# Moving the transposes of x between the scores and the output product in a decoupled cross-attention kernel

## The reference

```python
q = heads(x @ W_q);  k_t = heads(text @ W_k);  v_t = heads(text @ W_v)
probs_t = softmax(q k_t^T * scale)                       # over 73 text tokens
text_out = probs_t @ v_t
qsem = l2norm(probs_t @ text);  sem = qsem @ l2norm(ip)^T # over the 1024 context columns
probs_ip = softmax(q k_ip^T * scale + 0.5 * sem) * spatial_mask   # over 4 image tokens
out = (text_out + probs_ip @ v_ip) @ W_out + b_out + x
```

## Time and profile before

| | us |
|---|---|
| median of 3 runs (lowest, highest) | 1042.71 (1041.78, 1043.53) |
| the profiled execution | 1040.03 |
| span of its trace, first to last instruction | 1038.2 |
| TensorE busy | 981.1 |
| VectorE busy | 806.9 |
| ScalarE busy | 707.7 |
| GpSimd busy | 641.9 |
| busy time of all 16 DMA engines in queue q1 | 84.3% |

### The profile page before, as it was taken

One profiled execution on the slowest core, in us unless ns is written; L12 is line 12 of the kernel. 1 busy time (PEld: TensorE's weight loads), 2 busy tenths in 40 slices (PEclk: granted clock), 3 DMA queues, 4 the chain that ended last, 5 costly groups with the idle time before them and its releaser, 6 DMA issues.

```text
span 1038.2 us, 24562 instructions
## 1 busy us (share of the span) xinstructions
PE 981.1 (95%) x7604; PEld 791.6 (76%) x7604; DVE 806.9 (78%) x2401; ACT 707.7 (68%) x2315; POOL 641.9 (62%) x1899
## 2 busy tenths in 40 slices
PE   7986778999999999999999999999999999999877
PEld 5755666888877888888877888888878888888755
DVE  4375678888978788888878888888868888887851
ACT  1354778777677777777766777777767787777720
POOL 1112467777676677667666767767756677676750
PEclk9988999999999999999999999999999999999989
DMA  9845988979799998888899989798889989679852
GB/s 292 325 129 133 192 160 157 165 169 186 160 191 178 186 190 172 172 169 169 156 200 180 186 172 182 156 187 167 164 179 193 177 172 184 138 158 150 161 116 74
DMA packets 483871, 180.26 MB, mean 174 GB/s; under 512 B 449517, under 2 KB 461855, under 8 KB 483740
## 3 DMA queue, kind: packets, MB, share of 16 engines
q1 hardware_dynamic: 483708, 178.62, 84.3%
q10 hardware_dynamic: 32, 0.07, 0.0%
HBM read 42.34 MB, written 27.22 MB: 67 GB/s over the span
## 4 chain that ended last, share of the span: by engine, by line
PE 76%; DMA 5%; DVE 3%; ACT 2%; SPq 2%; issue 2%; POOL 1%; POOLq 0%; DVEq 0%; ACTq 0%
PE ps_O L1149 25%; PE ps_Q L1183 25%; PE ps_S L1122 12%; PE ps_U L1169 11%; DMA pts<-ph 5%; PE ps_M L1199 3%; ACT pr L905 2%; SPq L825 1%; SPq L795 0%; ACT ph L917 0%; DVE smax L1014 0%; DVE pr L1060 0%; DVE n L1072 0%; SPq L785 0%; DVE bias L1021 0%
## 5 line engine op out<-in xcount | busy, mean ns | idle before, releaser
L905 ACT ACTIVATE pr<-ps_S,bias 128x73 f32<-128x73 f32 x1280 | 290.1, 339 | 130.4 <-DVE bias L1021 129.8
L987 POOL TENSOR_TENSOR ph<-pr,ph 128x220 f16<-128x220 f32 (+1 forms) x640 | 273.6, 460 | 153.4 <-ACT ph L917 153.3
L1149 PE MATMUL ps_O<-wo_hi,aT 128*128 128x320 f16 x1280 | 297.2, 303 | 5.6 <-DVE x_in L1006 3.5
L1183 PE MATMUL ps_Q<-xT,wq_hi 128*128 128x512 f32 x800 | 282.4, 418 | 6.8 <-DVE qT L994 6.5
L917 ACT ACTIVATE ph<-pr 128x292 f16<-128x292 f32 x640 | 234.2, 440 | 5.1
L1149 PE MATMUL ps_O<-wo_lo,aT 128*128 128x320 f16 x640 | 193.4, 302 | 0.0
L1169 PE MATMUL ps_U<-xm,pts 128*128 128x110 f16 (+1 forms) x2560 | 159.7, 213 | 20.6 <-DMA pts<-ph 17.6
L1149 PEld LDWEIGHTS ps_O<-wo_hi,aT 128*128 128x128 f16 x1280 | 126.0, 98 | 64.1 <-DVE x_in L1006 4.1
L1183 PEld LDWEIGHTS ps_Q<-xT,wq_hi 128*128 128x128 f32 x800 | 147.8, 193 | 34.8 <-DVE qT L994 8.1
L1169 PEld LDWEIGHTS ps_U<-xm,pts 128*128 128x128 f16 (+1 forms) x2560 | 144.6, 98 | 38.6 <-issue 14.5
L1122 PE MATMUL ps_S<-kbd,qT 128*128 128x308 f32 x960 | 168.5, 311 | 5.2 <-ACT pr L905 5.1
(11 more groups left out here) (185 smaller groups left out, 1273.2 us busy)
## 6 DMA issues: line engine op xcount, KB each, us to landing
out_dram<-x_in SPq DMA_DIRECT2D x64, 320.0 KB, 2.6
x_in<-in_x_dram SPq DMA_DIRECT2D x56, 320.0 KB, 3.2
pts<-ph SPq DMA_TRANSPOSE x320, 3.4
aT<-in_L_xattn_W_k_dram SPq DMA_DIRECT2D x5, 512.0 KB, 8.7
w_ip<-in_L_xattn_W_k_ip_dram SPq DMA_DIRECT2D x1, 2560.0 KB, 11.6
w_v<-in_L_xattn_W_v_dram SPq DMA_DIRECT2D x1, 2560.0 KB, 19.5
w_ip<-in_L_xattn_W_v_ip_dram SPq DMA_DIRECT2D x1, 2560.0 KB, 9.4
x_in<-in_x_dram SPq DMA_DIRECT2D x2, 1280.0 KB, 12.4
```

Of the source, the lines that this page charges most:

```text
L905: last = nc.scalar.activation(pr[p % P_RING][:, j, h, :], sc[:, j, h, 0:T], ACT.Exp, bias=bias[p % 2][:, j, h:h + 1], scale=SCALE)
L987: nc.gpsimd.tensor_tensor(lo, full[:, :, t0:t1], one[:, :, 0, t0:t1], ALU.subtract).then_inc(pl_ready, 1)
L1149: last = nc.tensor.matmul(o_bank[half % 2][:, 0:HALF], stationary, moving, start=(k, a, b_) == O_MMS[0], stop=(k, a, b_) == O_MMS[-1])
L1183: last = nc.tensor.matmul(ps_Q[:], wq[a][:, c, k * P:(k + 1) * P], xT[(CC * i + c) % XT_RING][b_][:], start=(c, a, b_) == Q_MMS[0], stop=( ...
```

## The change

TensorE's transposes X move from the end of a step to the place right behind S and ahead of O. ScalarE and VectorE take them out of `ps_M` in the same step p instead of p+1. The chunks c = 3 and 4 are placed one step later in the table, so that their copies stay in the steps they were in; the chunks 0, 1, 2 keep their steps, so that their copies come a step earlier.

```diff
-    XT_AT = {-10: 0, -9: 1, -8: 2, -4: 3, -3: 4}
+    XT_AT = {-10: 0, -9: 1, -8: 2, -3: 3, -2: 4}
@@ scalar engine
-                for j, c in x_at(p - 1):
+                for j, c in x_at(p):
                     act.wait_ge(xT_ready, CC * j + c + 1)
@@ tensor engine, step p
                     last.then_inc(s_ready, 1)            # end of S
+                for j, c in x_at(p):
+                    if j == 0 and c < X_EARLY:
+                        continue
+                    if c == 0:
+                        pe.wait_ge(x_loaded[j % X_RING], ...)
+                    if j:
+                        if m_free is not None:
+                            pe.wait_ge(*m_free)
+                        m_free = xT_lo, CC * j + c + 1
+                    for q in range(SUB):
+                        last = nc.tensor.transpose(x_bank(j, c)[:, q * P:(q + 1) * P],
+                                                   x_in[j % X_RING][:, q, c * P:(c + 1) * P], ident[:])
+                    last.then_inc(xT_ready, 1)
                 for i, half, piece in out_at(p):         # O
...
                         last.then_inc(q_ready, 1)        # end of Q
-                for j, c in x_at(p):
-                    (the same block)
```

More of the change, by code:

```diff
@@ L1125, in _ @@
                     last.then_inc(s_ready, 1)
+                for j, c in x_at(p):
+                    if j == 0 and c < X_EARLY:
+                        continue
+                    if c == 0:
+                        pe.wait_ge(x_loaded[j % X_RING], 16 * (SUB * (j // X_RING + 1) if j % X_RING > 1 else SUB * (j // X_RING) + 1))
+                    if j:
[6 more added lines that the diff above has]
+                    last.then_inc(xT_ready, 1)
                 for i, half, piece in out_at(p):
```

## The result

The changed kernel takes 1032.39 us (median of 4, 1031.25 to 1034.81) against 1042.99 us (median of 4, 1041.78 to 1043.53): ratio 0.9912, 95% interval 0.9892 to 0.9931. It is 10.6 us faster where 1.8 were forecast. The profiled execution took 1031.25 us, with a span of 1029.5.

A forecast was written before the change was run, and what follows sets the result against it. TensorE bounds it, full from 180 to 940 us and often waiting from 97 to 180. Start -1.2, changes of batch -0.9, late S +0.3 make -1.8 us: 1042.7 to 1040.9 us, range 1037.3 to 1045.5.

The forecast's parts named there:

- The base: From 180 to 940 us: TensorE busy 752.2 of 760 us, its only sizeable wait U's for `pts`, 7.7 us.
- that execution lay 2.7 us under the median of the runs: Remark in the sum: the profiled execution took 1040.03 us, the median 1042.7.
- Rival B: Steps 1 and 7: new order makes GpSimd's instruction hold `bias`, S(63) waits 0.5 us, 7.5 us lost, 1048; chance 0.15.
- They miss each other by more than now: Argument against a slower kernel: in step 1 `bias` comes 0.09 us earlier while GpSimd isn't earlier.
- Gain 1: Start, 97 to 180 us: X and copies moved out of the chain gain 1.2 us, bounds 0 and 2.0.
- Gain 2: Changes of batch: X goes ahead of U's wait in steps 40 and 82, 0.44 us each, 0.9 us; bounds 0 and 0.9.
- a wait which I had priced at nothing: Tile load, needed 5 us earlier: if late by 1 or 2 us in step 80, X waits before a waiting U; nothing.
- What stayed hidden: Every tile: S loses cover, 0 to 0.1 us a tile; ScalarE's and VectorE's copies and the tile load cost nothing.
- the 0.3 put down: Step 66 to 67: S some 0.1 us late behind the exponentials in such tiles; 0.3 us in all, ends 0 and 1.5.
- 0.4 us of cover: Step 62 on ScalarE: free at 443.1 after X's copy and two others, `bias` comes at 443.54.
- Rival A: Start: earlier X shortens waits so one or two TensorE clock falls vanish, about 1 us each; 1038.2, chance 0.17.

The follow-up runs named there:

- before_no_reload: Kernel before without the loads of keys and values for batches 1 to 3 and TensorE's waits for them: 0.9924, 1035.3 us against 1042.6.
- before_psum3: Kernel before with `smax` in PSUM instead of SBUF only in steps that end in 3: 0.9949, 1036.5 us against 1041.3.
- the first two experiments: Both kernels rerun unchanged (0.9991, 0.9914); then chunks 0, 1, 2 a step earlier in the kernel before (1.0001), a step later in the changed one (0.9923).
- before_psum: Kernel before with `smax` in unused PSUM columns instead of SBUF in all steps: 0.9958, 1032.4 us against 1038.2.
- split_34: Only chunks 3 and 4 moved behind S, chunks 0, 1, 2 as in the kernel before: 1.0000 of the kernel before, and 0.9990 when run again.
- before_psum_all: Kernel before with `smax` in PSUM in all steps, run again on another chip: 0.9933, 1034.2 us against 1041.3.
- before_psum7: Kernel before with `smax` in PSUM instead of SBUF only in steps that end in 7: 0.9957, 1038.1 us against 1041.3.

## Why the prediction was wrong

**The base.** The step that failed is the first one: "TensorE is simply full, and its only wait of size is U's for `pts`", which made the long regime worth nothing. That held for the execution in the profile and not for the kernel. In other executions Q of step 7 waits 0.36 us for a `qT` that stands behind a held `bias`, in ten or eleven tiles, at 0.77 us a tile: 8 us that the sum had at nothing. Of the four profiles with this order and with `smax` in SBUF in every step, two have tiles of 55.5 us (1040.0 and 1037.1 us in all) and two of 56.3 (1044.4 us, and before_no_reload). There was a faint sign in the prediction itself, "that execution lay 2.7 us under the median of the runs"; but on the next chip single executions of the kernel before ran from 1038.2 to 1047.5 us, so 1040.0 was nothing unusual, and only a second profile could tell. The hold of step 7 is not the whole gain either: the execution of 1040.0 us, which has none, still took 7.6 us more than the changed kernel's median of 1032.4.

**Rival B, the right mechanism with the wrong sign.** It weighed the lock only as something that the change might switch on. The change switches it off. "They miss each other by more than now" was said of step 1, where it did not come true: the median distance from `bias` to GpSimd's instruction is 0.25 us in that profile and 0.20 after, and the changed kernel has three held there, in steps 41, 81 and 121. It came true in step 7, which nobody had measured: 0.04 us in step 77 before, 0.43 after. The price was taken by the wrong path too. I followed the held `bias` to `nd` and the next step's S, 0.5 us; it is Q of the same step that waits for `qT`, and 0.77 us a tile. That it costs in step 7 and not in step 3 goes with O, which has 11 matmuls in the one and 17 in the other, so that Q comes later; no run varies this.

**Gain 1, the start, 1.2 us.** Not confirmed. From S of step 0 to S of step 16 the profiles of the kernel before took 85.3, 85.5 and 86.2 us, those of the changed one 85.1, 85.5 and 82.9. A gain of a microsecond is possible, and smaller than the spread; the waits for `pts` in this stretch are 11.8 us after, in 13 waits, and were 10.6 in eleven. Lost, as the lower bound had it, or hidden.

**Gain 2, the changes of batch, 0.9 us.** Right in kind, too small. The three stretches took 177.7, 178.6 and 176.4 us in profiles of the kernel before (one held `bias` of step 7 in the second) and 173.6, 175.2 and 176.1 after: 2.6 us by the means. But a part of that is the clock. In each of the three profiles before, and in one of the three after, one stretch was granted 0.97, and these four took 59.8, 60.6, 60.3 and 60.2 us; those at the full clock took 57.3 to 59.8. Two stretches of the kernel before (the profile with 1037.12 us):

```profile
520.00:580.30 60.30, 57.58 (x453) 47.03 (x452) 46.46 (x144) 42.59 (x142) 39.07 (x118) 0.97 0.95 184
746.86:805.02 58.16, 56.35 (x452) 45.72 (x451) 47.74 (x144) 42.43 (x142) 39.09 (x118) 1.00 0.95 187
```

Counting full-clock stretches alone, the mean is 58.7 before and 58.1 after, 1.8 us for three. "As SP sets the time in such a stretch, only the last wait of each counts" is the sentence that fails. The chain of the kernel before goes in steps 80 and 82 from U's wait through Q and X into the next S and from there to the next transfer:

```profile
546.51 0.58 PE ps_U L1169 x8
547.09 1.92 PE ps_Q L1183 x8
549.02 0.44 PE ps_M L1199 x4
549.45 0.87 PE ps_S L1122 x6
...
554.18 3.98 DMA pts<-ph
...
558.21 0.58 PE ps_U L1169 x8
```

X at the end lies on this loop in both rounds shown, 0.44 us each, where the forecast counted one; X behind S is off it. Against that stands a wait which I had priced at nothing, for the load of the tile, in step 40 of the changed kernel:

```profile
315.87 0.66 PE L1138 MATMUL ps_M<-ident,x_in 128*128 128x128 f32 x4 [0.56 <-DMA x_in<-in_x_dram]
```

It did take the place of U's wait there, as the prediction says of step 80, and in step 120 it was 0.88 us.

**What stayed hidden.** As forecast or better. X costs 0.44 us behind S. In the changed kernel step 66 came out as forecast: the exponentials end at 464.91, the stopped TensorE starts S of step 67 at 465.05, and the step lasts 5.32 us. But that tile was the tightest of the kernel before; in the other quiet tiles S comes 0.25 us or more behind the exponentials, 0.1 us more than that start, and step 6 lasts 5.24 us. So 0.1 us of the 0.3 put down was spent. ScalarE in step 62 has the exponentials at 440.16 after an idle 0.47 us, where I had counted 0.4 us of cover:

```profile
438.43 0.60 ACT L874 ACTIVATE xT<-ps_M 128x512 fp32r<-128x512 f32 x1 [1.31 <-PE ps_M L1138]
...
440.16 1.82 ACT L905 ACTIVATE pr<-ps_S,bias 128x73 f32<-128x73 f32 x8 [0.47 <-DVE bias L1021]
```

**Rival A** got no support where it looked: the granted clock from 97 to 180 us is 0.94, 0.92 and 0.96 in three profiles of the kernel before and 0.94, 0.96 and 0.96 in three of the changed one. Over whole executions it does play a part. On the chip of before_psum3 the kernel before took 1044 to 1047 us (medians) where it was granted 0.982 and 0.983, 1040.6 at 0.985, and 1037 to 1039 at 0.987 and 0.988. The average of all executions is 0.9846 for the kernel before and 0.9862 for the changed one on the chip of the first two experiments, 0.9841 and 0.9862 on that of before_psum, which itself has 0.9871. Within one kernel 0.001 of clock goes with some 0.8 us (a line through the executions of all kernels, each from its own mean), so an estimate is that 1.5 us of the gain go with the clock. Whether the change keeps the clock up or was lucky in it is open.

**Shown, argued, open.** Shown: the held `bias` of step 7 makes tiles of 56.3 us, and the changed kernel's have 55.5; this is 8.5 of 9.4 us or more where there is no change of batch, in one profile of each. Shown: taking every hold away without touching the order gives 5.8 and 7.1 us in the kernel before, and on the one chip where both ran the change gave 6.3. Argued only: that this is the hold of step 7, that executions differ by who wins the race, and that the chips differ in how often; I have four profiles of that order with `smax` in SBUF, two of each kind. Open: why freeing step 3 alone gives 4.8 us, and why split_34, which never holds step 7 in its two profiles but once, gives 0 and 2 us. A hold in step 3 may be what brings the race of step 7 to the losing side; no profile shows it. It may also lengthen the changes of batch: the three take 174.9 us in before_psum and in before_psum_all and 177.0 in before_psum7. The 176.7 of before_psum3, which has no hold in step 3 either, don't speak against it: one of its stretches was granted 0.97 and took 60.6 us, the others 57.9 and 58.2. But single stretches at the full clock scatter over 2 us, and no run settles it. Nor does the race explain the spread of the executions: before_psum, with nothing held, still lies between 1029.4 and 1038.1 us, and the profiled execution of before_psum3, with tiles of 55.5, took 1041.2.

## What to carry to other kernels

One profile is one execution, and what it shows as costless may be what the others pay: two profiles of one kernel had tiles of 55.5 and of 56.3 us here. Take two or three before calling a regime full, and compare the granted clock of two executions before explaining what lies between them. Where two engines can hold each other, write down by how much they miss each other now, in each step, and not only whether a change could bring them together: a margin of hundredths of a microsecond is a cost that is paid in some executions. And if a small SBUF-to-SBUF operation is the one that is held, keeping its source in PSUM takes it out of the race at no cost that the profiles show (5.8 and 7.1 us gained here); the change of order gained 6.3 us beside the first of these, and the other order of GpSimd lost 27.

## What was not expected of the hardware

One instruction of 8 elements a partition decides 0.8% of the kernel (8.5 us, where no batch changes): `bias` takes 0.17 us alone and up to 1.22 us where GpSimd's 1.15 us instruction starts within 0.04 us behind it. In step 7 of the quiet tiles it was held at distances of 0.01 to 0.04 us, not each time, and never above, and an execution keeps to one outcome over nearly all its tiles: ten or eleven of fifteen in two profiles, none and one in two others. With its source in PSUM, all 160 took 0.166 to 0.168 us, GpSimd's instruction of 1.16 us as before. The rule of the lock (the Trainium skill, SBUF — State Buffer, "Who interferes with whom") names `tensor_scalar` among those that can contend with GpSimd when their operands allow a two-port mode. The traces agree: with `smax` in SBUF it was held, 24 of 160 in one profile, and with `smax` in PSUM none in three.
